# Even pairs of the selection select later, last context groups loaded ahead, and causal self attention begun in the preceding stage

## The reference, cut to what matters

```
scores = Q K^T / sqrt(32), -inf where the vision mask is off    # 4 heads, 4096 keys per batch
topv, topi = top_k(scores, 32);  probs = softmax(topv)
attn_mean = scatter(probs).mean(over heads);  c = attn_mean @ x_vision @ Wv
x = xt + FiLM(S4D(FiLM(layernorm(x), c))) + FFN(...), then layernorm     # x1b
x = x + CausalSelfAttention(layernorm(x))                                # a1, with rotary q, k
x = x + MXFP4_linear(layernorm(x))                                       # quantizer, in a1 too
```

## Time and profile before

| | us |
|---|---|
| median of 3 runs (2236.24 to 2239.41) | 2236.43 |
| the profiled execution | 2235.89 |
| its span | 2234.0 |
| busy: PE / DVE / ACT / POOL | 1806.8 / 1245.4 / 1026.2 / 759.8 |
| mean granted TensorE clock | 0.877 of 2.4 GHz |

### The profile page before, as it was taken

How to read it: one execution, slowest core, us unless ns; L and a number is a source line. 1 busy time by engine, 2 the same in 40 slices (tenths; PEclk the granted TensorE clock), 3 DMA queues, 4 the chain that set the end, 5 groups by cost and what they waited for, 6 DMA issues and landing times.

```text
span 2234.0 us, 34846 instructions
## 1 busy us (share of the span) xinstructions
PE 1806.8 (81%) x13676; PEld 1106.7 (50%) x13676; DVE 1245.4 (56%) x3075; ACT 1026.2 (46%) x1381; POOL 759.8 (34%) x669
## 2 busy tenths in 40 slices
PE   5969999999999987888697869767776568876775
PEld 2434554454445444565576425444553356664553
DVE  5142333423242301446586588999999957626675
ACT  1457667756765785212221345556455421013442
POOL 6243325432441420000120057777778712010000
PEclk7989999999999999999787656788877789988887
DMA  6657555664855450000200002132231240000000
GB/s 143 116 107 127 115 115 104 117 122 108 131 109 125 75 115 1 1 2 2 103 22 2 13 8 79 50 86 71 64 86 50 103 155 36 1 0 1 1 6 15
DMA packets 78046, 150.01 MB, mean 67 GB/s; under 512 B 15464, under 2 KB 63144, under 8 KB 71464
## 3 DMA queue, kind: packets, MB, share of 16 engines
q1 hardware_dynamic: 64304, 101.80, 16.2%
q0 software_dynamic: 12768, 42.59, 12.5%
q10 hardware_dynamic: 792, 3.17, 0.4%
HBM read 93.59 MB, written 2.62 MB: 43 GB/s over the span
## 4 chain that ended last, share of the span: by engine, by line
PE 49%; DVE 27%; ACT 11%; issue 5%; POOL 4%; DMA 3%; DVEq 0%; ACTq 0%; POOLq 0%; SPq 0%
PE R L112 31%; PE B L112 16%; ACT P L571 8%; DVE CA L1667 6%; DVE PM L1709 6%; DVE CA L1679 2%; DVE T L1681 2%; POOL KST L789 2%; PE B L178 1%; ACT PS L2284 1%; DMA CT<-in_ctxT 1%; DMA CN<-in_ctxn 1%; DMA KST<-OV 1%; POOL ACC L1789 1%; ACT RT L116 1%
## 5 line engine op out<-in xcount | busy, mean ns | idle before, releaser
L571 ACT ACTIVATE P<-R 128x1024 f32<-128x1024 f32 x512 | 506.8, 1026 | 217.1 <-PE R L112 181.8
L112 PE MATMUL R<-QS,KST 100*128 100x256 bf16 x2048 | 295.6, 276 | 61.1 <-ACT P L571 53.6
L112 PEld LDWEIGHTS R<-QS,KST 100*128 100x128 bf16 x2048 | 169.5, 98 | 224.6 <-ACT P L571 121.8
L200 POOL TENSOR_TENSOR LNrs<-LNve,pk_const 128x2 f32<-128x2 f32 x36 | 25.3, 703 | 503.8 <-DVE LNve L196 503.7
L1789 POOL TENSOR_TENSOR ACC<-ACC,PM 128x4096 f32<-128x4096 f32 x22 | 195.0, 8864 | 1.8
L112 PE MATMUL R<-OV,QT 32*128 32x512 f32 x512 | 180.1, 790 | 0.0
L789 POOL DMA_DIRECT2D KST<-OV x300 | 144.5, 490 | 72.2 <-PE R L112 55.7
L112 PE MATMUL R<-P,VP 128*32 128x256 f32 x2304 | 154.7, 385 | 0.3 <-ACT P L571 0.3
L601 DVE CAST OV<-RT 128x512 bf16<-128x512 f32 x64 | 27.5, 429 | 209.0 <-ACT RT L116 121.2
L1779 POOL TENSOR_TENSOR SM<-SM,NG 128x1 f32<-128x1 f32 x30 | 79.2, 2641 | 156.9 <-DVE PM L1709 156.9
L733 POOL CAST OV<-RT 128x512 bf16<-128x512 f32 x64 | 42.6, 665 | 258.7 <-DVE RT L604 258.6
(11 more groups left out here) (365 smaller groups left out, 3559.7 us busy)
## 6 DMA issues: line engine op xcount, KB each, us to landing
KST<-OV POOLq DMA_DIRECT2D x276, 128.0 KB, 10.9
CT<-in_ctxP SPq DMA_DIRECT2D x40, 768.0 KB, 4.5
CN<-in_ctxn SPq DMA_DIRECT2D x64, 384.0 KB, 3.4
CT<-in_ctxT SPq DMA_DIRECT2D x64, 192.0 KB, 2.5
KST<-OV SPq DMA_DIRECT2D x84, 128.0 KB, 10.1
KST<-in_ctxP ACTq DMA_DIRECT2D x4, 768.0 KB, 9.4
QS<-x_q POOLq DMA_DIRECT2D x24, 128.0 KB, 5.4
pk_a<-in_pk_a SPq DMA_DIRECT2D x1, 3014.0 KB, 11.0
```

What stands on the lines that cost most here:

```text
L112: return e.matmul(o, l, r, start=st, stop=sp, skip_group_check=True)
L571: e.activation(P[(32 * p + k0) % 3][:, :], ring.at(("s", p, k0))[:, :], ACT.Exp).then_inc(*EX.up((p, k0)))
```

## The change

Five edits.

1. In DVE's loop of the selection, `check` and both `select` of an even pair come after all 32 candidates of h = 0, not after 16. Odd pairs stay.
2. Context 7 (`ML`) has five CN buffers, three of them views of S0 behind x1c. SP loads groups 2, 3 and 4 of it ahead of the x1c load, when selection 14 has ended; groups 5 to 7 wait for the product five before, not two.
3. `a1_head`: norms, transposes and copies of batches 0 and 1 for self attention run in x1b, in steps 9 and 10 of batches 2 and 3, their buffers XN, XT being views of F and Gi; the q and k products of batch 0 come at PE's end of x1b, into R[0] and R[1]. `begin` in a1 is q, k, ks, v of batch 0, of which PE does ks and v only.
4. In a1 DVE norms batches 2 and 3 two iterations earlier (u = 2 and 6, behind the quantizer job, ahead of the wait for ACT).
5. At the end, `project(3)` comes ahead of `q_turn(2)`.

```diff
+            CN += [two(S0[:, spec["x1c"][0] + 768 * i:spec["x1c"][0] + 768 * i + 768], 4) for i in range(3)]
...
+            def place_of(m, g):
+                return g % (5 if m == ML else 2)
...
-                            if h == 0 and g == 15 and 0 <= n - 2 < NP:
+                            if h == 0 and g == (31 if n % 2 == 0 else 15) and 0 <= n - 2 < NP:
...
+                    elif m < ML:
+                        e.wait_ge(*M.at(("c", m, g - 2)))
+                    elif g < 5:
+                        e.wait_ge(*V.at(("sel", NP - 2, 1)))
+                    else:
+                        e.wait_ge(*M.at(("c", m, g - 5)))
...
                     if n == NP + 1:
                         e.wait_ge(*V.at(("sel", NP - 2, 1)))
+                        for g in (2, 3, 4):
+                            context_in(ML, g)
                         load(e, "x1c", t_x1c, LC1)
...
+        def a1_head(w, x1b):
+            XN, XT = ([two(x1b[nm].rearrange("p a n -> p (a n)")[:, 512 * i:512 * i + 512]) for i in range(2)] for nm in ("F", "Gi"))
+            bank = {("q", 0): R[0], ("k", 0): R[1]}
+            def norm(e, b):
+                norm_stats(e, 2 + b, xrows(b), V, ("ve", b))
+                e.wait_ge(*G.at(("rs", b)))
+                norm_apply(e, 2 + b, xrows(b), XN[b], V, ("xn", b))
+            def turn(e, b, ps):
+                bank["xt", b] = ps
+                e.wait_ge(*V.at(("xn", b)))
+                transposes(e, ps, XN[b]).then_inc(*M.up(("xt", b)))
+            def product(e, p):
+                for t4 in range(4):
+                    for kc in range(2):
+                        ins = mm(e, bank[p, 0][:, t4 * 256:t4 * 256 + 256], w["W" + p][:, kc, t4 * 128:t4 * 128 + 128], XT[0][:, kc, :], kc == 0, kc == 1)
@@ x1b, tensor @@
                     elif s in (9, 10):
                         f2 = s - 9
+                        if f2 == 1 and b >= 2:
+                            ps, free = bank.take(("head", b), (head["S"], ("xt", b - 2)))
+                            for sg, k in free:
+                                e.wait_ge(*sg.at(k))
+                            head["turn"](e, b - 2, ps)
...
+                e.wait_ge(*LL["a1"].at("a1"))
+                e.wait_ge(*S.at(("in", NB - 1, 1)))
+                e.wait_ge(*head["S"].at(("xt", 0)))
+                head["product"](e, "q")
+                head["product"](e, "k")
@@ x1b, scalar @@
+                        if f2 == 1 and b >= 2:
+                            e.wait_ge(*M.at(("y", NB - 1)))
+                            head["copy"](e, b - 2)
@@ x1b, vector @@
+                    elif s == 9 and b >= 2:
+                        e.wait_ge(*M.at(("xf", NB - 1)))
+                        e.wait_ge(*V.at(("x", b - 2)))
+                        head["norm"](e, b - 2)
@@ x1b, gpsimd @@
+                    elif s == 9 and b >= 2:
+                        head["root"](e, b - 2)
...
-            begin = [(0, p) for p in ("norm", "xt", "q", "k", "ks", "v")] + [(1, p) for p in ("norm", "xt")]
+            begin = [(0, p) for p in ("q", "k", "ks", "v")]
...
-                    if turned_at(u) is not None:
+                    if u < NU and turned_at(u) is not None:
                         q_turn(turned_at(u))
                 project(NB - 1)
+                q_turn(NB - 2)
                 q_product(NB - 2)
@@ a1, vector @@
                     for b, p in pieces(u - 1):
-                        piece(b, p)
+                        if p != "norm":
+                            piece(b, p)
...
                         for job in quant(u):
                             quantise(*job)
+                        for b, p in pieces(u + 1):
+                            if p == "norm":
+                                piece(b, p)
                         e.wait_ge(*S.at(("ex", u, 1)))
```

More of the change, by code:

```diff
@@ L1449, in stage_x1a @@
             LM1, MUL, MRD = dsig("text_mask"), dsig("x1_mask"), dsig("x1_mask_rows")
-            CNL = [dsig(f"cn{i}") for i in range(2)]
+            CNL = [dsig(f"cn{i}") for i in range(5)]
+            ML = 2 * NB - 1
             reg = held
@@ L1819, in sync @@
                     for g in gs[0:2 if n % 2 == 0 else 4]:
-                        context_in(m, g)
+                        if m < ML or not 2 <= g < 5:
+                            context_in(m, g)
                     for ch in range(8):
@@ L1823, in sync @@
                             keys["sync"](e, *rekeyed(n, ch))
-                        if m is not None and n % 2 == 0 and ch in (2, 4):
+                        if m is not None and n % 2 == 0 and ch in (2, 4) and m < ML:
                             context_in(m, gs[1 + ch // 2])
@@ L1830, in sync, with root, copy, stage_x1b @@
                         e.wait_ge(*V.at(("sel", NP - 2, 1)))
+                        for g in (2, 3, 4):
+                            context_in(ML, g)
                         load(e, "x1c", t_x1c, LC1)
             return dict(tensor=tensor, vector=vector, scalar=scalar, gpsimd=gpsimd, sync=sync, slots=(ring, bank))
-        def stage_x1b(c, late, w2):
+        def a1_head(w, x1b):
+            XN, XT = ([two(x1b[nm].rearrange("p a n -> p (a n)")[:, 512 * i:512 * i + 512]) for i in range(2)] for nm in ("F", "Gi"))
+            M, V, S, G = sig("a1_head_product"), sig("a1_head_norm"), sig("a1_head_copy"), sig("a1_head_root")
+            bank = {("q", 0): R[0], ("k", 0): R[1]}
[3 more added lines that the diff above has]
+                norm_apply(e, 2 + b, xrows(b), XN[b], V, ("xn", b))
+            def root(e, b):
+                e.wait_ge(*V.at(("ve", b)))
+                norm_root(e, 2 + b).then_inc(*G.up(("rs", b)))
+            def turn(e, b, ps):
+                bank["xt", b] = ps
+                e.wait_ge(*V.at(("xn", b)))
+                transposes(e, ps, XN[b]).then_inc(*M.up(("xt", b)))
+            def copy(e, b):
+                e.wait_ge(*M.at(("xt", b)))
+                acopy(e, XT[b], two(bank["xt", b][:, :])).then_inc(*S.up(("xt", b)))
+            def product(e, p):
+                for t4 in range(4):
+                    for kc in range(2):
+                        ins = mm(e, bank[p, 0][:, t4 * 256:t4 * 256 + 256], w["W" + p][:, kc, t4 * 128:t4 * 128 + 128], XT[0][:, kc, :], kc == 0, kc == 1)
+                ins.then_inc(*M.up((p, 0)))
+            return dict(XN=XN, XT=XT, M=M, S=S, bank=bank, norm=norm, root=root, turn=turn, copy=copy, product=product)
+        def stage_x1b(c, late, w2, head):
             w = dict(pack(c, "x1b", OV)[1])
@@ L2077, in stage_x1b, with stage_a1 @@
             return dict(tensor=tensor, vector=vector, scalar=scalar, gpsimd=gpsimd, sync=sync, slots=(ring, bank))
-        def stage_a1(c, views, wq):
+        def stage_a1(c, views, wq, head):
             w = views
@@ L2085, in stage_a1 @@
             for i in range(2):
-                for nm, sh in (("XN", [128, 2, 256]), ("XT", [128, 2, 256]), ("K1", [128, 4, 256]), ("K2", [128, 4, 256]),
+                nb["XN", i], nb["XT", i] = head["XN"][i], head["XT"][i]
+                for nm, sh in (("K1", [128, 4, 256]), ("K2", [128, 4, 256]),
                                ("QT", [128, 4, 256]), ("KT", [128, 4, 256]), ("VN", [128, 2, 272]), ("PS", [128, 4, 384]),
@@ L2148, in piece @@
                         if p == "q":
-                            e.wait_ge(*S.at(("xt", b)))
+                            e.wait_ge(*(head["S"] if b < 2 else S).at(("xt", b)))
                         for t4 in range(4):
@@ L2239, in q_product @@
                     ins.then_inc(*QM.up(("y", b)))
-                e.wait_ge(*LL["a1"].at("a1"))
-                for b, p in begin:
+                for b, p in begin[2:]:
                     piece(b, p)
@@ L2535, in build @@
         late = {nm: pack(ctx, nm) for nm in ("a1", "qf")}
+        head = a1_head(late["a1"][1], pack(ctx, "x1b", OV)[1])
         with ExitStack() as c:
-            stages.append(stage_x1b(c, late, x1c))
+            stages.append(stage_x1b(c, late, x1c, head))
         with ExitStack() as c:
-            stages.append(stage_a1(c, late["a1"][1], late["qf"][1]))
+            stages.append(stage_a1(c, late["a1"][1], late["qf"][1], head))
         def tensor(e):
```

26 lines of the change are left out of this document (11 added, 15 removed).

## The result

The changed kernel takes 2197.88 us (median of 4 runs, 2195.46 to 2203.82) against 2236.34 of the kernel before in the same session: ratio 0.9831, 95% interval 0.9806 to 0.9855, 38.5 us faster. 2197 was forecast. The profiled execution took 2203.82 (span 2202.0), the slowest of the four: its stages before the selection, which the change leaves alone, ran 7.7 us longer than in the profile of before. So from here on times are differences between two markers of one profile, which this offset does not enter.

A forecast was written before the change was run, and what follows sets the result against it. DVE bounds the selection, stalled by POOL in even pairs; in the last stage engines wait for each other in turn. From 2236.43 us, 9.6 - 0.6 + 19.8 + 10.7 = 39.5 gives 2197, range 2188 to 2207.

The forecast's parts named there:

- the stall of even pairs: Selection, pairs 4 to 14 even: DVE's select stands still until POOL's addition into ACC ends, 7.56 us against a 4.48 median.
- Selection 9.6: Selecting even pairs later gains 9.6 us, with mask conversions and a query norm slowed beside POOL; ends 5 and 17.
- the rival of only two-input selects waiting: Selection: only the two-input select waits for POOL, so 14.2 + 1 to 3 us instead of 9.6; chance 0.22.
- That doesn't move: 0: Selection, pair 10: pair 11's select already waits 1.9 us for ACT, fed from POOL's sum of pair 9; gain 0.
- the one sign of being wrong that came up: Selection: ACT waiting longer for line 1709, the mask-and-multiply of the select, would show the forecast wrong.
- Context groups -0.6: Context 7 loads: (7,0) put back 2.9 us, later products gain 3.1, clock loss 0.8; net -0.6, ends -4 and +3.
- Head 19.8: Attention begun in x1b: first MX of the last stage at 2004.9 instead of 2024.67, gain 19.8 us; ends 17 and 21.
- Norms 10.7: Last stage: norms of batches 2 and 3 two iterations earlier gain 10.7 us together; ends 6 and 13.
- The first, 5.6: Last stage, MX(4): 8.4 us sooner without wait and norm, less 1.2 and 1.6, gives 5.6.
- The second, 5.1: Last stage, MX(8): 7.2 us gained, less 2.0 for the norm's new place in iteration 6, gives 5.1.
- Last edit 0: End of last stage: project(3) starts some 1.5 us sooner but delays batch 2's work; 0, ends -1 and +1.5.
- that rival: Attention stage pays less, 20 to 24 us instead of 30.5, total about 2205; chance 0.16.

The follow-up runs named there:

- half way: The kernel before with the selection of even pairs after 24 candidates instead of 16; 2227.86 us, one run.
- first three groups: The changed kernel with groups 0 to 2 of context 7 loaded ahead of x1c, not 2 to 4; 2184.95 us, ratio 0.9764 to before.
- select only: The kernel before with the first edit alone, even pairs selecting after all 32 candidates; 2226.18 us, ratio interval 0.9921-0.9961.
- head only: The kernel before with the third edit alone, attention begun in x1b; 2215.22 us, ratio interval 0.9868-0.9925.
- norms only: The kernel before with the fourth edit alone, norms of batches 2 and 3 two iterations earlier; 2227.28 us, ratio interval 0.9928-0.9965.
- after: The changed kernel with all five edits; 2197.88 us, ratio 0.9831 to the kernel before.

## Why the prediction was right, point by point

- **What bounds it, the stall of even pairs.** Shown, by half way above all: the stall is what is left of POOL's addition.
- **Selection 9.6; it gave 12.4.** Pairs 4, 8, 12 and 14 gave 1.7, 1.7, 2.8 and 3.1, for 1.5, 1.5, 2.8 and 2.7. Pairs 0 and 2 gave 0 as taken, though a conversion and a norm met POOL there too (1.51 and 1.58): pair 3 waits 2.4 us for ACT in any case. The lock on the mask and the query norm was the right choice between the bounds, and with it the rival of only two-input selects waiting falls (it also needed 15 or more). The Trainium skill, SBUF — State Buffer, Who interferes with whom, gave that rule, and the trace agrees, 1.51 to 1.57 against 0.20 us for a conversion from 8 bits. The step that failed is "That doesn't move: 0" for pair 10. POOL's sum of pair 9 didn't move, but the work behind it ran at 0.94 instead of 0.50 of the clock: 3.5 us. Pair 6 went the other way, -0.4 for 1.1, by the same mechanism. It also made the one sign of being wrong that came up, selects that wait longer for ACT's copies (4.2 us for 1.9): S came free no later, but TensorE at 1.2 GHz filled it later.
- **Context groups -0.6; -0.7 in the profile, -1.1 by the kernel with the old loads.** The term was right, and its parts were not: the load of (7,0) put its product back by 4.6 us from pair 15's select, for 2.9 (its wait grew by 3.7 and the transposes ahead of it took 0.9 longer), and the products behind it gained 3.9 for 2.3 (3.1 less the estimated 0.8 for the clock, of which the second product shows 0.4, 2.47 for 2.07). That these two errors cancel is luck. That the wait is set by the loads ahead of it in SP's queue, first three groups shows.
- **Head 19.8; it gave 20.3**, and 20.4 alone. The barrier opened by TensorE and each step behind it came as worked out.
- **Norms 10.7; they gave 8.1.** The first, 5.6, measured 5.5. The second, 5.1, measured 2.6 against before, and 4.9 between kernels whose projection of batch 0 ran equally slow. Its own two parts came as worked out: from MX 7 to 8 7.1 us shorter for 7.2, from MX 6 to 7 1.8 longer for 2.0. Iterations 4 and 5 are 0.9 and 1.7 us longer. The 1.7 is the slow projection, since iteration 5 is as long in select only (16.04); the 0.9 stays open. What failed is no step of the sum but what it left out: that a projection at 3.72 in the one profile read could be one at 5.41 in the next.
- **Last edit 0; it costs 1.0** beside a slow projection, the only kind seen in both orders. The end of the range was named (-1) and the reason too, transpose and product of batch 2 behind the projection; the choice of the middle was wrong. C, which I took as unchanged, gave 0.7.
- **The sum** was 39.5 and the stretches give 39.7, with 2.8 too little in the selection and 2.6 too much in the norms: a part of the agreement is luck. Attention as a whole gave 28.0 of the 30.5 (20.3 + 5.5 + 2.6 + 0.7 - 1.05), above the 20 to 24 of that rival. The edits alone give 10.9, 21.8 and 9.8, in all 42.5; the second and fifth cost 1.1 and 1.0, which leaves 40.4 against 38.5 measured, a difference that does not tell from none when the medians of before itself lie between 2235.9 and 2241.7.

## What to carry to other kernels

When an engine stands still for a lock, moving the long operation is half of the work: look at what small operation then comes to lie beside the same neighbour, and move that too. It was worth 6.5 us here, 4.5 of them the lock and 2.0 TensorE's clock, against 9.6 that the move itself was forecast to bring. Put ahead of a large transfer what is needed first, not what happens to have a buffer: against the old loads, three groups ahead of x1c cost 1 us when they were 2 to 4 and gained 6 when they were 0 to 2. And judge a small term by the distance of two markers in one profile, and only between runs in which TensorE's clock at that place was the same.

## What the hardware showed unexpectedly

TensorE's clock at a given place repeats. Behind the seven waits for POOL's sum the granted clocks were 0.50, 0.66, 1.00, 0.56, 0.50, 0.70, 1.00 in the profile of before and the same within 0.02 in head only and norms only, whose selection is the same code; 0.50, 0.67, 0.50, 0.70, 0.94, 0.50, 0.90 in after and, within 0.02, in the three kernels on it with the same selection. So a stretch of 8 us at 1.2 GHz with TensorE busy throughout is no accident of a run, and an edit can turn it on or off by moving work by 1 to 3 us. In a1 the projection of batch 0 took 3.72, 5.1 to 5.4 or 6.7 us by kernel, and B followed it: 47.97 and 50.21 without the fourth edit, 45.3 and 46.2 with it. Nothing tried here turns the clock into time reliably: 36 filling transposes kept it at 0.80 or more behind all seven waits and gained nothing, as TensorE then idled elsewhere and went on at 0.50; 22 had 0.50 behind two waits and the shortest selection.
